# Expansion's first high mixing stage moved into TensorE's path products, with three moves in VectorE's order

## The reference, cut to what matters

```python
x = x + ssm(layernorm(x), in_proj_w, conv_w, conv_b, x_proj_w, A_log, D, out_proj_w)
h = einsum('bsd,dh->bsh', layernorm(x), W_exp) + b_exp          # 256 -> 1024
h = butterfly(h, up_weights, 1024)                              # 10 stages
h = gelu(h + up_bias)
h = butterfly(h, down_weights, 1024)
x = x + einsum('bsh,hd->bsd', h, W_con) + b_con + down_bias

def butterfly(y, weights, dim):
    for stage in range(10):
        s = 2 ** stage; nb = dim // (2 * s)
        a, b = y.reshape(nb, 2, s)[:, 0], y.reshape(nb, 2, s)[:, 1]
        w = weights[stage].reshape(nb, s, 2, 2)
        y = stack([w[..., 0, 0] * a + w[..., 0, 1] * b, w[..., 1, 0] * a + w[..., 1, 1] * b])
```

## Time and profile before

| | us |
|---|---|
| median of 3 runs (543.35 to 543.48) | 543.41 |
| the profiled execution's own time | 543.8 |
| its span in the trace | 542.1 |
| TensorE busy | 516.0 (95%) |
| VectorE busy | 416.8 (77%) |
| ScalarE busy | 307.0 (57%) |
| GpSimd busy | 93.3 (17%) |

### The profile page before, as it was taken

One profiled execution on the slowest core, in us unless ns is written; L12 is line 12 of the kernel. 1 busy time (PEld: TensorE's weight loads), 2 busy tenths in 40 slices (PEclk: granted clock), 3 DMA queues, 4 the chain that ended last, 5 costly groups with the idle time before them and its releaser, 6 DMA issues.

```text
span 542.1 us, 8227 instructions
## 1 busy us (share of the span) xinstructions
PE 516.0 (95%) x3012; PEld 422.5 (78%) x3012; DVE 416.8 (77%) x892; ACT 307.0 (57%) x537; POOL 93.3 (17%) x88
## 2 busy tenths in 40 slices
PE   4989999998999999999999999999999999889997
PEld 3756776776887788878888788888888789578886
DVE  4778999888984999489975999489956986576542
ACT  2777883794249622875269722964278514951242
POOL 4040200220211202140211211030213021122020
PEclk9995988999999999999999999999999999999999
DMA  9652511200112001210112002110021001200011
GB/s 223 134 28 3 83 39 41 66 16 2 39 40 76 6 2 50 69 41 1 40 40 81 0 2 79 54 28 2 0 79 42 1 1 39 81 0 1 1 40 39
DMA packets 42635, 21.75 MB, mean 40 GB/s; under 512 B 26435, under 2 KB 41027, under 8 KB 42596
## 3 DMA queue, kind: packets, MB, share of 16 engines
q1 hardware_dynamic: 39956, 17.57, 13.9%
q10 hardware_dynamic: 2640, 3.67, 2.4%
HBM read 16.78 MB, written 4.46 MB: 39 GB/s over the span
## 4 chain that ended last, share of the span: by engine, by line
PE 58%; DVE 20%; ACT 9%; issue 9%; POOL 2%; DMA 1%; DVEq 0%; ACTq 0%; POOLq 0%
PE wide L715 11%; PE acc L877 11%; PE wide L866 9%; PE wide L855 9%; DVE xc L1516 5%; PE wide L829 4%; DVE state L1621 3%; PE small L705 3%; PE wide L840 2%; ACT xc L1186 2%; DVE diag_sum L1639 2%; DVE diag L1635 2%; DVE hid_low L1533 1%; PE wide L725 1%; PE small L735 1%
## 5 line engine op out<-in xcount | busy, mean ns | idle before, releaser
L1146 ACT ACTIVATE hid_f<-wide,bias_up 128x512 f32<-128x512 f32 x64 | 43.9, 686 | 160.5 <-PE wide L866 157.5
L1516 DVE SCALAR_TENSOR_TENSOR xc<-xi,taps,xc 128x512 f32<-128x512 f32 x96 | 96.2, 1007 | 4.5 <-ACT xc L1177 2.3
L877 PE MATMUL acc<-w_down_high,hid_high 128*128 128x256 f32 x256 | 73.7, 288 | 3.5 <-DVE hid_low L1533 3.4
L877 PE MATMUL acc<-w_down_high,hid_low 128*128 128x256 f32 x256 | 72.0, 281 | 0.0
L877 PE MATMUL acc<-w_down_low,hid_high 128*128 128x256 f32 x256 | 72.0, 281 | 0.0
L1533 DVE TENSOR_TENSOR hid_low<-hid_f,hid_high 128x512 fp32r<-128x512 f32 x64 | 47.4, 743 | 15.5 <-ACT hid_high L1259 15.2
L855 PE MATMUL wide<-w_out,xc 128*128 128x256 f32 x256 | 58.4, 388 | 0.7 <-DVE xc L1660 0.5
L715 PE MATMUL wide<-xnT_ln1T_high,w_in_high 128*128 128x512 f32 x128 | 56.7, 443 | 0.0
L877 PEld LDWEIGHTS acc<-w_down_high,hid_high 128*128 128x128 f32 x256 | 48.3, 188 | 10.2 <-issue 6.6
L866 PE MATMUL wide<-xnT_ln2T_high,w_up_high 128*128 128x512 f32 x128 | 54.2, 424 | 1.7 <-DVE xnT_ln2T_low L1527 1.7
L855 PEld LDWEIGHTS wide<-w_out,xc 128*128 128x128 f32 x256 | 49.2, 194 | 7.8 <-issue 1.1
(11 more groups left out here) (193 smaller groups left out, 1035.3 us busy)
## 6 DMA issues: line engine op xcount, KB each, us to landing
x_res<-in_L_attn_x_dram SPq DMA_DIRECT2D x9, 512.0 KB, 3.5
c_near<-c_of_tokens SPq DMA_DIRECT2D x8, 512.0 KB
x_ln<-in_L_attn_x_dram SPq DMA_DIRECT2D x7, 512.0 KB, 3.6
out_dram<-x1b_xn SPq DMA_DIRECT2D x7, 512.0 KB, 2.9
xc<-in_L_attn_in_proj_w_dram ACTq DMA_DIRECT2D x2, 512.0 KB, 7.1
xc<-in_L_ffn_W_exp_dram ACTq DMA_DIRECT2D x1, 1024.0 KB, 11.1
x1b_xn<-in_L_ffn_W_con_dram ACTq DMA_DIRECT2D x1, 1024.0 KB, 15.0
raw_out<-n_L_attn_out_proj_w_dram ACTq DMA_DIRECT2D x1, 512.0 KB, 7.7
```

What stands on the lines that cost most here:

```text
L877: last = pe.matmul(acc[:, c, :], hid[h][:, j % HRING, c * P:(c + 1) * P], w_down[w][:, j, 0:DM], start=j == 0 and c % 2 == 0 and n == 0, s ...
L1146: ins = act.activation(out_ap, in_ap, how.pop("func"), **how)
L1516: ins = dve.scalar_tensor_tensor(xc[u % BATCH][:, e, :], xi[:, e, tap:tap + TILE], taps[:, e, tap:tap + 1], xc[u % BATCH][:, e, :], ALU.mu ...
```

## The change

High stage 0 of expansion is no longer a mixing stage of its own. GpSimd writes the 16 weight columns of that stage onto the diagonals of 16 matrices (`weights_on_diagonals`, one select of 16x128 columns, into the tile `mixed`). A path product is then path matrix times diagonal matrix instead of path matrix times identity, 16 of them instead of 8 (steps 8 and 9), and `up_low` adds two products in its bank, one for each of the two blocks that the stage mixes. MIXES of expansion keeps stages 1 and 2; `pathT` moves from `x_res` to the tile of the low weights. The `high_w` loads of expansion go ahead of tile 1's load and have a semaphore of their own. From there on all preparation steps have a number higher by one, and TensorE and ScalarE run one more of them ahead of input projection 7. `load_for_residual(0)` waits for the normalisation of tile 1 instead of the last `up_low`.

VectorE's moves: the wait for `zeroed` goes from `constants` into `softplus(0)`; in `first_phase` the statistics of tile 2 go behind gate 1 and its normalisation behind gate 3; in `to_first_outputs` (used in phase 1 alone) `convolve(v, 0)` goes from the front to behind gate 3, ahead of `low_hidden(p, 3)`.

```diff
@@ -320,11 +320,13 @@
...
         low_loaded = [sem(f"low_loaded{i}") for i in range(2)]
-        CONV_LOADS, SMALL_LOADS = 4, 2 * HIGH + 4
+        high_loaded = sem("high_loaded")
+        CONV_LOADS, SMALL_LOADS = 4, HIGH + 4
         masks_made = sem("masks_made")
...
         perm_made = sem("perm_made")
+        diags_made = sem("diags_made")
         rates_exp = sem("rates_exp")
@@ -339,7 +341,8 @@
...
         perm = hid_f32[:, :, :].rearrange(flat)[:, 0:LOW * P].rearrange("p (s q) -> p s q", q=P)
-        pathT = x_res[:, :, :].rearrange(flat).rearrange("p (g j) -> p g j", j=P)
+        pathT = low_w[0][:, :].rearrange("p (n j) -> p n j", j=P)
+        diags = mixed[:, :, :].rearrange(flat)[:, 0:2 * HID].rearrange("p (n j) -> p n j", j=P)
         partial = x1[:, :, :].rearrange(flat)
@@ -364,6 +367,7 @@
...
             [("pathT", 0, 0), ("pathT", 1, 0)],
+            [("pathT", 2, 0), ("pathT", 3, 0)],
             [("up_low", 0, 0), ("up_low", 1, 0)],
@@ -416,7 +420,7 @@
...
-        MIXES = {UP: [(0, mixed, wexpT), (1, wexpT, mixed), (2, mixed, wexpT)],
+        MIXES = {UP: [(1, mixed, wexpT), (2, wexpT, mixed)],
                  DOWN: [(2, raw_con, con_mixed), (1, con_mixed, raw_con), (0, raw_con, con_mixed)]}
@@ -447,16 +451,19 @@
...
             sp.dma_start(raw_x, x_proj_w).then_inc(w_loaded["x_proj"], 16)
+            def load_high(i, signal):
+
+                for s in range(HIGH):
+                    sp.dma_start(high_w[i][:, s, :, :], (up_weights, down_weights)[i][LOW + s].rearrange("(q p) o i -> p q (o i)", p=P)).then_inc(signal, 16)
+
+            load_high(UP, high_loaded)
             sp.dma_start(x_res[:, :, :], tokens(1)).then_inc(early_loaded, 16)
...
                 sp.dma_start(bias_raw[:, n, :], row.partition_broadcast(P)).then_inc(s_loaded, 16)
-            for i, weights in enumerate((up_weights, down_weights)):
-                for s in range(HIGH):
-                    sp.dma_start(high_w[i][:, s, :, :],
-                                 weights[LOW + s].rearrange("(q p) o i -> p q (o i)", p=P)).then_inc(s_loaded, 16)
+            load_high(DOWN, s_loaded)
             load_low(sp, DOWN, down_weights, range(0, 4))
@@ -467,7 +474,7 @@
...
                 if u == 0:
-                    sp.wait_ge(made, number[("up_low", HB - 1, 0)] + 1)
+                    wait(sp, norm1, 1, GR)
                 sp.dma_start(x_res[:, :, :], tokens(u)).then_inc(res_loaded.handle, 16)
@@ -555,6 +562,15 @@
...
             ins.then_inc(perm_made, 1)
+
+            def weights_on_diagonals(stage):
+
+                pool.affine_select(out=diags, in_=high_w[UP][:, stage, :, :].rearrange("p q w -> p (q w)").unsqueeze(2)
+                                   .to_broadcast([P, 2 * HB, P]), compare_op=ALU.is_equal, fill=0.0, base=0,
+                                   pattern=[[0, 2 * HB], [-1, P]], channel_multiplier=1).then_inc(diags_made, 1)
+
+            pool.wait_ge(high_loaded, 16 * HIGH)
+            weights_on_diagonals(0)
             rstd_of(1, 0, var1, rstd1)
@@ -658,19 +674,24 @@
...
                         wait_taken(pe, ("low", UP, q))
+                    pe.wait_ge(diags_made, 1)
                     for q in range(4):
-                        g = 4 * i + q
-                        last = pe.transpose(bank[:, q * P:(q + 1) * P], paths[UP][:, g * P:(g + 1) * P], ident[:, :])
+                        n = 4 * i + q
+                        g = n // 4 * 2 + n % 2
+                        last = pe.matmul(bank[:, q * P:(q + 1) * P], paths[UP][:, g * P:(g + 1) * P], diags[:, n, :],
+                                         start=True, stop=True)
                 elif name == "up_low":
...
                         pe.wait_ge(s_loaded, 16 * SMALL_LOADS)
-                        wait_taken(pe, ("pathT", 0, 0))
-                        wait_taken(pe, ("pathT", 1, 0))
-                    last = pe.matmul(bank[:, 0:W1], pathT[:, i, :], wexpT[:, i, :], start=True, stop=True)
+                        for q in range(4):
+                            wait_taken(pe, ("pathT", q, 0))
+                    for n in range(2):
+                        last = pe.matmul(bank[:, 0:W1], pathT[:, 2 * i + n, :], wexpT[:, i // 2 * 2 + n, :],
+                                         start=n == 0, stop=n == 1)
                 elif name == "w_up":
-                    wait_mixed(pe, UP, HIGH - 1, HB - 1)
+                    wait_mixed(pe, UP, 1, HB - 1)
                     for q in range(4):
-                        last = pe.transpose(bank[:, q * P:(q + 1) * P], wexpT[:, 4 * h + q, i * P:(i + 1) * P], ident[:, :])
+                        last = pe.transpose(bank[:, q * P:(q + 1) * P], mixed[:, 4 * h + q, i * P:(i + 1) * P], ident[:, :])
                 else:
@@ -930,10 +951,11 @@
...
                 off_diagonal(0)
+                prepare(13)
                 in_projection(1, 7)
-                prepare(13)
+                prepare(14)
                 ssm_output(0)
-                prepare(14)
+                prepare(15)
                 transposes(2, "ln1T", x_ln, norm1)
@@ -1041,13 +1063,13 @@
...
                 if place == "in 5":
-                    prepare(15)
+                    prepare(16)
                 elif place == "in 6":
-                    prepare(16)
+                    prepare(17)
                 elif place == "products":
...
                 elif place == "up 1":
-                    prepare(17)
+                    prepare(18)
                 elif place == "up 2":
@@ -1123,6 +1145,7 @@
...
                 if n == 0 and i == UP:
+                    act.wait_ge(high_loaded, 16 * HIGH)
                     for g in range(HB - 2, HB):
@@ -1291,12 +1314,12 @@
...
                 copy_z(1, 6)
+                prepare(13)
                 copy_z(1, 7)
...
                 scale_blocks(UP, 0)
-                scale_blocks(UP, 1)
                 high_parts(2, "ln1T")
@@ -1359,13 +1382,13 @@
...
                 if place == "ln2T":
-                    scale_blocks(UP, 2)
+                    scale_blocks(UP, 1)
                 elif place == "z 5":
-                    prepare(15)
+                    prepare(16)
                 elif place == "z 6":
-                    prepare(16)
+                    prepare(17)
                 elif place == "gelu 1":
-                    prepare(17)
+                    prepare(18)
@@ -1449,7 +1472,6 @@
...
                                        rates[:, :].unsqueeze(1).to_broadcast([P, NB, NS]), ALU.mult))
-                dve.wait_ge(zeroed, 2)
@@ -1489,16 +1511,18 @@
...
                 stage, source, target = MIXES[i][n]
+                if n == 0 and i == UP:
+                    dve.wait_ge(high_loaded, 16 * HIGH)
                 for g, _, high, _, weight in mixing(i, stage):
...
                                              ALU.mult, ALU.add).then_inc(mixed_up[i], 1)
-                if n == HIGH - 1:
+                if n == len(MIXES[i]) - 1:
                     wait_mixed(dve, i, n, HB - 1)
-                if (i, n) == (UP, HIGH - 1):
-                    dve.tensor_tensor(bias_up[:, :], wexpT[:, :, DM], up_bias_sb[:, :], ALU.add)
+                if (i, n) == (UP, 1):
+                    dve.tensor_tensor(bias_up[:, :], mixed[:, :, DM], up_bias_sb[:, :], ALU.add)
@@ -1562,6 +1586,8 @@
...
                                   ALU.mult).then_inc(dB_ready.handle, 1)
+                if u == 0:
+                    dve.wait_ge(zeroed, 2)
                 dve.tensor_tensor(dA[:, :, 0:NS], rates[:, :].unsqueeze(1).to_broadcast([P, GR, NS]),
@@ -1742,15 +1768,14 @@
...
                 multiply_short_paths(DOWN)
-                first_stats(2)
                 gate(0, 0)
                 gate(0, 1)
-                first_normalise(2)
+                first_stats(2)
                 gate(0, 2)
                 gate(0, 3)
+                first_normalise(2)
                 multiply_whole_paths(DOWN)
                 add_blocks(UP, 0)
-                add_blocks(UP, 1)
                 low_parts(2, "ln1T")
@@ -1760,7 +1785,6 @@
...
                 v, r, p = u + 1, u + 2, u - 1
-                convolve(v, 0)
                 diagonal_times_c(u)
@@ -1775,8 +1799,9 @@
...
                 gate(u, 3)
+                convolve(v, 0)
+                low_hidden(p, 3)
                 convolve(v, 1)
-                low_hidden(p, 3)
                 convolve(v, 2)
@@ -1857,7 +1882,7 @@
...
                 if place == "softplus":
-                    add_blocks(UP, 2)
+                    add_blocks(UP, 1)
                 elif place == "weighed":
...
                 elif place == "assembled":
```

## The result

The changed kernel takes 549.85 us in the median (549.6 to 551.71, 4 executions), the kernel before beside it 543.44 (543.35 to 543.48): 1.0123 times the time, 95% interval 1.0103 to 1.0143, so 6.4 us slower. The forecast was 550.5. The profiled execution of after took 551.71 us (span 550.0); it is the longest of the four, so the two traces differ by 7.9 us where the medians differ by 6.4.

What follows compares the result with a forecast made beforehand. VectorE's gates, about 2.2 us behind TensorE, held the out projection, whose start moves the end one for one. Gates 4.8 plus convolution 2.3 gave 7.1 us on 543.8: 550.9, median 0.4 lower, 550.5 us; range 546.5 to 553.5.

Steps and rivals of the forecast that it cites:

- Part 1: TensorE ahead of tile 0's output products: added path and up_low products 5.48 us, less a 0.80 gap, net 4.68.
- Part 2: Mixing at 88.56: 3.2 us leave VectorE, which then waits for TensorE's bank at the residual; worth 0, other bound 3.2.
- Part 3: First-phase gates: normalisation put last delays tile 2's transposes, queued ahead of the out projection, which starts at 92.1: +4.8 us.
- Part 4: Phase 1: the moved convolution gains 0 where it leaves and passes 2.32 us into phase 2: +2.3, bounds 0 and 2.3.
- rival (c): Convolution absorbed: an early phase 1 TensorE wait shrinks by as much as the late one grows; 548.2 us, 15%.
- Part 5: Kernel start: later wait for zeroed tiles, GpSimd's select and earlier high_w loads cost 0; loads up to +1.8 us.
- Rival (f): GpSimd's select at the start comes late, so rstd and all behind it slip: 551 to 553 us, 2%.
- the clock rivals: Two cases on half-clock stretches near the output products and out projection: kinder clock (15%) or harsher clock (12%).
- (a): Kinder clock: one or both slow stretches at output products and out projection go; 548.8 down to 546.9 us, 15%.
- (b): Harsher clock: TensorE idles ahead of the out projection, the slow stretch lasts through twice as much: +1.9, 552.4 us, 12%.
- Rival (d): VectorE alone spaces the first phase; output products start under 2.2 us behind 73.62, mixing's 3.2 us go: 540.2, 7%.
- Rival (e): The parts of the change cancel over the whole kernel: 543.4 us, 4%.

Runs made afterwards that it cites:

- e10: The changed kernel run again without any edit, to see whether its time follows the granted clock: 549.95 us (1.0118 of before).
- e9: The changed kernel with TensorE's transposes of tile 2 moved from ahead of the out projection to between its two halves: 551.63 us (1.0150 of before).
- e1: The changed kernel with convolve(v, 0) put back at the front of to_first_outputs: 547.46 us (1.0079 of before).
- e3: The changed kernel with both VectorE moves undone (convolution; statistics and normalisation), diagonal products kept: 543.79 us (1.0013 of before).
- e2: The changed kernel with statistics back ahead of gate 0 and normalisation between gates 1 and 2: 548.17 us (1.0082 of before).
- e4: The kernel before without expansion's high stage 0, that mixing left out with nothing in its place: 542.65 us (0.9975 of before).
- e5: The kernel before with only convolve(v, 0) of phase 1 moved behind gate 3: 545.78 us (1.0044 of before).
- e11: The kernel before with only the start part: early high_w loads, GpSimd's select with TensorE's wait for it, later wait for zeroed: 544.12 us (1.0009).
- e6: The kernel before with only statistics moved behind gate 1 and normalisation behind gate 3: 544.42 us (1.0014 of before).
- e12: The kernel before with contraction's short paths behind gate 3, whole paths behind the second norm, some low products behind the out projection; rerun for trace: 544.68 us (1.0018).

## Why the prediction came out

**Part 1, the products: the mechanism right, the size too small.** Predicted 4.68, measured 5.15 (70.23 for 65.08 behind the first `rstd`), just inside its own range of 4.4 to 5.2. The other traces with all the products lie above it: 5.27 (e10), 5.29 (e9), 5.36 (e1), 5.47 (e3) and 5.90 (e2, whose first path group ran at half clock, 3.58 us). The two groups of path products take 55.10 - 53.33 = 1.77 us and 1.81, so 3.58 instead of 3.24, and the four groups of `up_low` 6.37 instead of 6.08 (the first 62.98 - 61.36 = 1.62). A quarter of a microsecond of waiting for ScalarE's copy is left of the 0.80 (the [0.25 <-ACT low_w L1140] above). What I had not seen: the first path group now waits 1.35 us for VectorE's `paths`, and still starts 0.77 us earlier than before, since the two-row low products ahead of it (45.71) took 1.98 us in this execution and 3.78 in that of before (45.64). From the path group to the output products lie 25.54 us, before 19.62, which is 5.9 more; the early start hid 0.8 of it. So it was in part luck that this trace fell inside the range.

**Part 2, the mixing worth 0: right in the full kernel, too low for the kernel before.** VectorE's two waits at the residuals, 3.42 us, are the 3.2 us that left. By e4 its removal alone brings 1.3 us (0.8 to 2.0); the part of that which the changed kernel could still use was not measured.

**Part 3, the move at the gates: the mechanism right, the size depends on the clock.** Predicted: first gate 82.7, normalisation 90.2, out projection 92.1 (+4.8). In the profiled execution: 83.58, 91.05, 93.60 (+6.15). The chain from the gate to the normalisation is exact (7.47, predicted 7.5). The excess has two parts. The first gate is 0.9 later than predicted: 0.6 because the output products start at 78.87 and not 78.3, and 0.3 because it comes 4.71 us behind them and not 4.4, with half-clock time among them (the state instructions 2.61 us for 1.97). And the eight transposes, which I had put at some 0.6 us behind the normalisation, took 2.21 at half clock, where e9 has 1.04. In e10's trace the same term is +4.23. The two traces stand on either side of 4.8.

**A small gain behind the out projection was not in the sum.** From the out projection to the first `w_down`, after needs 0.63 us less than before, in three pieces: to the x projection 8.58 us instead of 8.76 (93.60 to 102.18), from there to the first `w_up` 16.00 instead of 16.18, from there to `w_down` 10.29 instead of 10.56. The chain that ended last gives 8.45 for the out projection, since it counts from the end of the transposes, 93.81, and not from the first instruction's start at 93.60:

```profile
93.81 8.45 PE wide L876 x32
102.25 1.87 PE wide L746 x8
```

**Part 4, the convolution: size right, place half wrong.** Predicted 2.3, measured 2.26 in the trace of after, 2.28 in that of e5 and 2.4 in the times between after and e1. Of the two bounds it is the upper. The TensorE wait for `w_down_low` stays at 1.0 us in all of them, so nothing was given back early; rival (c) falls. The place is told with e5; the sign that was named for it, a wait of over 1 us at `down` of block 6, did not come.

**Part 5, the start: 0 to 0.5 (e11).** Rival (f) falls: the select takes 2.01 us, in the lower half of what its 5.4 us bound allowed.

**Sum.** In the trace of after: 6.15 - 0.63 + 2.26 = 7.8 (predicted 7.1); in that of e10: 4.23 - 0.67 + 2.26 = 5.8; in the medians 6.4. The forecast lies between two executions of the same kernel, and each trace misses it, by 0.7 and by 1.3 us: that it came within 0.7 us of the median owes something to luck. Of the clock rivals, (a) is what e10's trace shows (its output products ran at full clock), (b) did not make it slower: the out projection behind the 1.89 us wait took 8.65 us in after and 8.61 in e10, not longer than the 8.83 of before. Whether that wait brings the slow stretch about is open. All four traces with the transposes waiting (1.89 us in after, e1 and e10, 2.44 in e6) have an out projection of 8.6 to 8.8 us, and e2 and e3, without the wait, 7.15 and 7.14; but before, e4 and e11 have 8.7 to 8.8 without it, and e12 has 7.14 behind a wait of 1.96 us. The rule of the Trainium skill that I had weighed for (b) ("TensorE: Matmul & The Clock Gate", What's actually happening: the throttled state is the default and activity releases it) agrees with the 0.50 of the window from 90 to 94, where TensorE was busy for 2.40 of 4.00 us. It does not give the price: the half-clock stretch lay on the transposes and took no more of the out projection than before. Rival (d), faster, fails at the point that it named: the output products start 5.2 us later, not less than 2.2. Rival (e), the parts cancel, is false for the change; but something like it holds for e3, and I had no term for it. With the moves undone, in e3, the output products start 5.5 us later than before (70.55 for 65.08), the first gate and the out projection only 2.0 (80.80 for 78.81), and its 32 instructions take 7.14 us at full clock instead of 8.83. TensorE's chain in e3:

```profile
88.97 7.14 PE wide L876 x32
```

So the diagonal products with the shorter mixing cost nothing that the times can tell (by the interval of e3 -0.2 to +1.6 us), though TensorE has 5 us more to do: part of it lay in VectorE's shadow ahead of the gates, and the rest was paid back by a half-clock stretch that did not come. That payment isn't sure: e3's executions run from 543.1 us at a mean clock of 0.987 to 547.3 at 0.978.

**What stays open.** Why e9's timed executions were 3.5 to 6 us above its profiled one, and more generally what decides in a given execution whether a half-clock stretch falls on the output products. e2 and e3, and after and e10, differ in it without any difference in the program ahead of it. In the six traces with all the diagonal products it goes with an earlier difference: where the low products at 45 us took 3.78 us (e1, e3, e9, e10), TensorE did not wait for `paths` and the output products ran at full clock; where they took 1.98 and 2.27 us (after, e2), it waited 1.35 and 2.38 us for `paths`, and the output products lay partly at half clock. In the kernels with the products of before this does not hold (before itself has 3.78 us and slow output products, e5 1.98 and fast ones), so it is a lead and not a cause.

## What to carry to other kernels

Work that is moved from one engine to another must be priced by who ends last at that very place, and an order that was written for the old balance has to be looked at again afterwards: the two VectorE moves cost 6.1 of the 6.4 us. By the traces this is because the normalisation that they put last feeds transposes that stand ahead of the critical product in TensorE's queue (though the times of e9, with the transposes out of the way, don't confirm it), and because the convolution went from where VectorE waited to where TensorE waits for VectorE; a part, some 1.5 us of the out projection in each pair of traces, is half-clock time. Before taking work off an engine, leave it out altogether once and time that (e4: 1.3 us for 3.2 us of mixing); if that is less than what the substitute costs where it lands, the substitute can't win. And look for the next ceiling behind the one that is being raised, here ScalarE's and VectorE's chain at 104 us, which took back the 1.8 us by which e12 came early to phase 1.

## What the runs showed of the hardware

- The same program places its half-clock stretches differently from one execution to the next. The 16 output products took 3.03 us in after and 2.05 in e10:

```profile
79.19 2.05 PE L829 MATMUL wide<-m_mat,x_tok 128*128 128x128 f32 x16
90.25 1.83 PE L726 MATMUL small<-ident,x_ln 128*128 128x128 f32 x8 [1.89 <-DVE x_ln L1450]
91.88 8.61 PE L876 MATMUL wide<-w_out,xc 128*128 128x256 f32 x32
```

- Where they fall matters where TensorE sets the pace. The kernel before takes 543.0 to 544.5 us whatever its mean clock (0.978 to 0.994), and in the trace of e5 the output products at full clock (2.05 us for 3.64) leave the first gate where it was (71.79 for 71.75 behind the first `rstd`); e3, which differs from before in the preparation and the start, varies over 4 us.
- VectorE's normalisation of tile 1 took 3.02 us in after for the four instructions that took 1.38 in the earlier trace rows. It now runs while GpSimd zeroes its tiles (29.54 to 32.60 us), which it had waited for until the change; e11, with the same order at the start, has 3.03 us, and e5, with the old order, 1.38. That GpSimd's work is the cause was not tested by itself:

```profile
29.72 3.02 DVE L1450 TENSOR_SCALAR x_ln<-x_res,mean_var,rstd 128x256 f32<-128x256 f32 x4
```

- A GpSimd select of 2048 columns took 2.01 us, where one of 128 took 0.34: 6 times the time for 16 times the columns.
